# A last tile routed by expert in a second phase, in place of eight dense expert blocks over it

## The reference, cut to what matters

```
x = x + xattn(layernorm(x), ctx)          # x: 1024 x 128, ctx: 6404 x 128
n = layernorm(x)                          # 1024 tokens, 128 wide
expert_id = argmax(n @ wr + br)           # 8 experts
h = gelu(n @ w1[e] + b1[e])               # 128 -> 512, for the token's expert e
y = h @ w2[e] + b2[e]                     # 512 -> 128
out = x + y                               # only the chosen expert's y counts
```

## Time and profile before

| | before |
|---|---|
| median of the runs | 234.51 us |
| profiled execution, its own time | 234.7 us |
| span of that execution | 233.0 us |
| TensorE busy | 200.8 us, 86% |
| VectorE busy | 180.4 us, 77% |
| ScalarE busy | 157.9 us, 68% |
| GpSimd busy | 126.6 us, 54% |

### The profile page before, as it was taken

The page is one execution under the profiler, slowest core; times in us unless marked ns, Lnnn a source line. Parts: engine busy times, 40 slices in busy tenths (PEclk is TensorE's granted clock), DMA queues, the critical chain, the costliest instruction groups (busy, mean ns, idle before and its releaser), DMA issues.

```text
span 233.0 us, 5011 instructions
## 1 busy us (share of the span) xinstructions
PE 200.8 (86%) x1837; PEld 151.4 (65%) x1837; DVE 180.4 (77%) x395; ACT 157.9 (68%) x249; POOL 126.6 (54%) x177
## 2 busy tenths in 40 slices
PE   0289969999999999979989999899992899799970
PEld 0133436776866777746656777699981899789960
DVE  2999797697998997997995999957848437567770
ACT  2752899399399698699596799789332355766630
POOL 3695819708906808958608957655302730027783
PEclk9999985799999999999999999999996569999995
DMA  6999979979999999999989999989991559999100
GB/s 208 381 259 258 221 239 249 225 192 191 232 180 227 260 220 271 231 200 240 230 207 274 207 249 230 211 180 212 234 284 47 191 191 314 366 370 344 43 21 0
DMA packets 142958, 51.78 MB, mean 222 GB/s; under 512 B 121172, under 2 KB 140773, under 8 KB 142934
## 3 DMA queue, kind: packets, MB, share of 16 engines
q1 hardware_dynamic: 142000, 50.08, 92.8%
q0 software_dynamic: 784, 1.38, 1.7%
q10 hardware_dynamic: 150, 0.00, 0.0%
HBM read 10.74 MB, written 3.75 MB: 62 GB/s over the span
## 4 chain that ended last, share of the span: by engine, by line
PE 41%; DVE 23%; issue 13%; DMA 11%; POOL 6%; ACT 4%; SPq 1%; POOLq 0%; DVEq 0%; ACTq 0%
DMA PT<-Phl 9%; DVE S L798 6%; PE psX L1073 6%; PE psS L1055 5%; PE psS L1053 5%; PE psS L1054 5%; POOL out_x L606 5%; PE psO L1073 4%; DVE Phl L815 4%; PE psX L1075 3%; ACT S L649 3%; PE psO L1075 2%; PE psS L1279 2%; DMA S<-in_x 2%; PE psX L1084 2%
## 5 line engine op out<-in xcount | busy, mean ns | idle before, releaser
L649 ACT ACTIVATE S<-S,negb 128x1024 f32<-128x1024 f32 x48 | 55.0, 1145 | 17.5 <-DVE negb L806 17.5
L798 DVE TENSOR_SCALAR_CACHE_REDUCE S<-psS 128x1024 f32<-128x1024 f32 x48 | 58.2, 1216 | 9.9 <-PE psS L1055 9.8
L815 DVE TENSOR_TENSOR Phl<-S,Phl 128x1024 f16<-128x1024 f32 x38 | 51.5, 1354 | 5.3 <-ACT Phl L664 5.2
L531 POOL TENSOR_TENSOR Phl<-S,Phl 128x256 f16<-128x256 f32 x40 | 26.4, 691 | 52.2 <-ACT Phl L664 52.2
L664 ACT CAST Phl<-S 128x1024 f16<-128x1024 f32 x48 | 50.2, 1045 | 5.6 <-DMA PT<-Phl 4.2
L1053 PE MATMUL psS<-qT,gh 128*128 128x512 f16 x96 | 37.6, 392 | 5.6 <-DVE gl L776 3.0
L1073 PE MATMUL psO<-qn,PT 128*128 128x256 f16 x204 | 37.7, 279 | 0.7 <-DMA PT<-Phl 0.7
L1073 PE MATMUL psX<-qn,PT 128*128 128x256 f16 x204 | 36.4, 273 | 2.0 <-DMA PT<-Phl 2.0
L1055 PE MATMUL psS<-qT,gl 128*128 128x512 f16 x96 | 37.7, 393 | 0.0
L1054 PE MATMUL psS<-qT,gh 128*128 128x512 f16 x96 | 37.7, 393 | 0.0
L1075 PE MATMUL psO<-qn,PT 128*128 128x128 f16 x204 | 36.2, 223 | 0.0
(11 more groups left out here) (239 smaller groups left out, 426.3 us busy)
## 6 DMA issues: line engine op xcount, KB each, us to landing
PT<-wp SPq DMA_DIRECT2D x8, 512.0 KB, 6.0
stageT<-in_ctxT SPq DMA_DIRECT2D x6, 512.0 KB, 7.3
qn<-wp SPq DMA_DIRECT2D x6, 512.0 KB, 6.5
wp<-in_w SPq DMA_DIRECT2D x4, 512.0 KB, 4.8
stageT<-in_w SPq DMA_DIRECT2D x4, 512.0 KB, 4.8
rows_by_expert<-stageT SPq DMA_DIRECT2D x4, 385.5 KB, 5.3
PT<-Phl SPq DMA_TRANSPOSE x48, 4.2
S<-rows_by_expert SPq DMA_DIRECT2D x2, 258.0 KB, 5.9
```

The costliest lines, as they stand in the source:

```text
L531: last = nc.gpsimd.tensor_tensor(lo[:, r], slot(t, e)[:, r], hi[:, r], ALU.subtract)
L649: nc.scalar.activation(slot(t, e), slot(t, e), ACT.Exp, bias=negb[:, t:t + 1], accum_out=Lp[:, t * NG + e:t * NG + e + 1]).then_inc(exp_do ...
L798: nc.vector.tensor_scalar(out=into, in0=bank(u, n)[:, 0:into.shape[1]], scalar1=1.0 / GS, scalar2=None, op0=ALU.mult, op1=ALU.max, accum_o ...
L815: nc.vector.tensor_tensor(lo, slot(t, e), hi, ALU.subtract).then_inc(low_done, 1)
```

## The change

The dense blocks are removed. Tile 7 is dispatched like the others, but in a second phase, since its routing is known later. The first phase is as before. Then TensorE counts tile 7's choices on top of those of the first seven tiles, VectorE works out how many further blocks each expert now needs (`extra`), which rows of tile 7 fit into free rows of the blocks that are there and which go to added blocks behind them (`pos7`), and a second table of block owners (`bexp_all`). GpSimd sends tile 7 with an eighth scatter. There are NB = 8 + 8 - 1 = 15 blocks, all dispatched, and TensorE's loop has 15 instead of 22. SyncE now fetches four blocks' weights ahead (the first phase settles their owners) instead of two, then waits for the second phase (`experts_ready` 2), loads the other eleven registers, waits for both scatters' landings and reads the rows. The copy of tile 7 to a high and low half is gone, as are the constant `pick` and tile 7's own output DMA.

```diff
-    NB = TA + E - 1
-    NBLK = E + NB
-    FIRST = 2
+    NB = T + E - 1
+    FIRST = 4
...
             for b in range(FIRST):
                 fetch(b)
-            sp.reg_load(expert_reg[FIRST:NB], bexp[0:1, FIRST:NB])
+            sp.wait_ge(experts_ready, 2)
+            sp.reg_load(expert_reg[FIRST:NB], bexp_all[0:1, FIRST:NB])
...
             sp.wait_ge(rows_sent, 16 * TA)
+            sp.wait_ge(last_sent, 16)
             block_rows(0, 0, D, rows_landed)
             block_rows(1, 0, D, rows_landed)
...
+            pool.wait_ge(x2n_ready, H + 1)
+            pool.wait_ge(pos7_ready, 1)
+            pool.indirect_dma_start(out=xs, ..., in_=pay[:, TA, :], in_offset=None).then_inc(last_sent, 16)
...
             act.wait_ge(x7T_in_psum, 1)
-            nc.scalar.copy(xTp[:, 0, NB, :], x7T_psum).then_inc(x7T_high, 1)
-            act.wait_ge(x7T_low, 1)
             nc.scalar.copy(x2T[:, TA * P:N], x7T_psum).then_inc(x7T_ready, 1)
...
+            dve.wait_ge(router7_in_psum, 1)
+            io, first = best(router7_psum, TA, T)
+            nc.vector.tensor_tensor(oneh[:, TA:T, :], io, first, ALU.is_equal).then_inc(chosen7_ready, 1)
+
+            dve.wait_ge(ranks7_in_psum, 1)
+            link(...)    # 12 linked instructions of 1 to 64 columns: nall, extra, ahead, shift, place, over
+            nc.vector.tensor_copy(pos[:, TA:T], posf[:, TA:T]).then_inc(pos7_ready, 1)
+            link(...)    # 6 more, three of them on 120 columns: opened, worth, hit, fix
+            nc.vector.tensor_scalar(bexp_all[:, :], fix[:, :], float(E - 1), None, ALU.min).then_inc(experts_ready, 1)
...
+            for t in range(TA):
+                nc.tensor.matmul(both7_psum..., ones16[:, :], oneh[:, t, :]...broadcast_to([P, 2, E]), ...)
             pe.wait_ge(x2n_ready, H + 1)
             nc.tensor.transpose(x7T_psum, x2n[:, TA, :], idf[:, :]).then_inc(x7T_in_psum, 1)
...
+            pe.wait_ge(chosen7_ready, 1)
+            nc.tensor.matmul(rank7_psum, before[:, :], oneh[:, TA, :], ...)
+            nc.tensor.matmul(count7_psum, ones16[:, :], oneh[:, TA, :], ...).then_inc(ranks7_in_psum, 1)
...
             pe.wait_ge(w_low, T)
+            turn(0)
             up(0)
-            router_last()
+            turn(1)
             up(1)
-            for b in range(NBLK):
-                if b == E - 2:
-                    turn(0)
+            for b in range(NB):
                 for g, (s0, _) in enumerate(BATCHES):
-                    if g >= 2 and b == E + s0 - 5:
+                    if g >= 2 and b == s0 - 5:
                         turn(g)
-                if b + 2 < NBLK:
+                if b + 2 < NB:
                     up(b + 2)
-                if b == E - 2:
-                    turn(1)
                 down(b)
```

More of the change, by code:

```diff
@@ new lines, in _ @@
+            link(nc.vector.tensor_reduce(out=nall[:, :], in_=more[:, :, :], axis=AX.X, op=ALU.add))
+            link(nc.vector.tensor_tensor(extra[:, :], nall[:, :], nblk[:, :], ALU.subtract))
+            link(nc.vector.tensor_tensor(below[:, :, :], tri[:, :, :],
+                                         extra[:, :].unsqueeze(1).broadcast_to([P, E, E]), ALU.mult))
+            link(nc.vector.tensor_reduce(out=ahead[:, :], in_=below[:, :, :], axis=AX.X, op=ALU.add))
+            link(nc.vector.scalar_tensor_tensor(out=shift[:, :], in0=ahead[:, :], scalar=eblk[:, E - 1:E],
+                                                in1=eblk[:, :], op0=ALU.add, op1=ALU.subtract))
@@ new lines, in _ @@
+            link(nc.vector.tensor_tensor(place[:, :], rank7_psum, sblk[:, :], ALU.add))
+            link(nc.vector.tensor_tensor(over[:, :], place[:, :], eblk[:, :], ALU.is_ge))
+            link(nc.vector.tensor_tensor(over[:, :], over[:, :], shift[:, :], ALU.mult))
+            link(nc.vector.tensor_tensor(place[:, :], place[:, :], over[:, :], ALU.add))
+            link(nc.vector.tensor_tensor(place[:, :], place[:, :], oneh[:, TA, :], ALU.mult))
+            link(nc.vector.tensor_reduce(out=posf[:, TA:T], in_=place[:, :], axis=AX.X, op=ALU.add))
@@ new lines, in _ @@
+            nc.vector.tensor_copy(pos[:, TA:T], posf[:, TA:T]).then_inc(pos7_ready, 1)
+            link(nc.vector.tensor_scalar(opened[:, :], ahead[:, :], eblk[:, E - 1:E], None, ALU.add))
+            link(nc.vector.scalar_tensor_tensor(out=worth[:, :], in0=iota_e[:, :], scalar=-float(E), in1=extra[:, :],
+                                                op0=ALU.add, op1=ALU.mult))
+            link(nc.vector.tensor_tensor(hit[:, :, :], opened[:, :].unsqueeze(1).broadcast_to([P, NB, E]),
+                                         slot_no[:, :, :], ALU.is_equal))
@@ L1004, in finish @@
                 half, t = psY[b % RING][:, 0:D], yt[:, b % RING, :]
-                if b >= E:
-                    nc.vector.tensor_tensor(yf[:, b - E, :], half, t, ALU.add).then_inc(y_ready, 1)
-                    return
-                nc.vector.scalar_tensor_tensor(out=y7[:, b, :], in0=half, scalar=mask[:, b:b + 1], in1=t,
-                                               op0=ALU.mult, op1=ALU.add).then_inc(y_ready, 1)
-            for b in range(NBLK):
+                nc.vector.tensor_tensor(yf[:, b, :], half, t, ALU.add).then_inc(y_ready, 1)
+            for b in range(NB):
                 for g, (s0, _) in enumerate(BATCHES):
@@ L1209, in _ @@
             pe.wait_ge(chosen_ready, 1)
-            nc.tensor.matmul(rank_psum, before[:, :], oneh[:, :, :].rearrange("p t e -> p (t e)"),
+            nc.tensor.matmul(rank_psum, before[:, :], oneh[:, 0:TA, :].rearrange("p t e -> p (t e)"),
                              start=True, stop=False, skip_group_check=True)
```

155 lines of the change are left out of this document (71 added, 84 removed).

## The result

| | before | with the change |
|---|---|---|
| first set: median (executions) | 235.0 us (4) | 238.06 us (4), 237.85 to 239.54 |
| ratio, 95% interval | | 1.0137 [1.0092, 1.0183] |
| profiled execution, own time / span | 234.7 / 233.0 us | 238.18 / 236.4 us |
| four later sets of the same kernels | | 1.0101 [1.0045, 1.0157], 1.0022 [0.9993, 1.0051], 1.0076 [1.0036, 1.0115], 0.9990 [0.9955, 1.0025] |

What follows compares the result with a forecast made beforehand. TensorE's work after the blocks' start was taken as the bound: first `up` 197.55 + blocks 24.15 + transposes 1.2 + end wait 1.5 + clock 2.9 = 227.3 against 226.66, +0.65, so 235.2 us (range 233.6 to 237.0).

Steps and rivals of the forecast that it cites:

- the wait: On SyncE before the first read of rows: read at 192.9 us, not 191.3, 2.9 us later than before.
- the load itself: SyncE's second register load: 4.5 us for eleven registers, from 0.12 us plus 0.40 per register.
- the loss by the low clock: TensorE's first blocks at 1.2 GHz: half of 5.8 us lost, 2.9 us, against 4.35 before.
- Transpose to second table: From tile 7's transpose ending at 180.60 us through routing and VectorE's chain: `pos7` at 186.2, second owner table at 187.8.
- What does hold the rows is the load of registers: On SyncE: the register load, from 187.9 to 192.4 us, not the eighth scatter, decides when rows are read.
- lands at about 191.3: GpSimd's eighth scatter: starts at 188.82 us and lands at about 191.3, 1.3 us later than the seventh.
- The clock: TensorE at the first blocks: starts at 1.2 GHz, rises to 2.4 GHz 5.8 us later, by 203.4 us.
- rival 3: At the first blocks: clock rises early, 3.8 us after the first `up`, 1.9 us lost, 234.2 us; chance 0.12.
- The base: The profiled execution of the kernel before: last matmul ending at 226.66 us, against which the sum of 227.3 gave +0.65.
- No wait of TensorE from there: In the blocks, once the clock is at 2.4 GHz by 203.4 us: TensorE never waits, last matmul at 227.3.
- Rival 4: Rows or weights come late, tightest at `turn(2)`, rows landing 204.5 us, wanted 205.8; 3 us worse costs 1.7, 236.9; chance 0.05.

Runs made afterwards that it cites:

- before_again: The kernel before, unchanged, run again for a second trace: 234.19 us, ratio 1.0017.
- before_less_constants: The kernel before without the two GpSimd affine_selects of the constant `pick`: 234.62 us, ratio 1.0021.
- before_laid_out_as_after: The kernel before with two tables allocated in the changed kernel's larger sizes, so later addresses match it; no instruction changed: 234.93 us, ratio 1.0026.
- after_again: The changed kernel, unchanged, run again for a second trace: 236.31 us, ratio 1.0101 to the kernel before.
- after_third: The changed kernel, unchanged, run once more for the spread of its executions: 235.62 us, ratio 1.0022 to the kernel before.
- after_busy_up_to_first_block: The changed kernel with 45 unread matmuls before the first transposes of rows and 5 more between those and the first block: 234.82 us, ratio 0.9991.
- after_tensore_kept_busy: The changed kernel with 40 unread matmuls in TensorE's idle stretch before the first transposes of rows: 237.24 us, ratio 1.0056 to the kernel before.

## Why the prediction was wrong

The size of the change was near (+0.65 forecast, +0.9 over the later sets), in part by luck; the number on record was not, and five of its steps were off, two of them against each other. The step that failed first is the wait: not the load of registers but the scatter decided when the rows were read. Two terms were mis-sized on top of it: the load itself (4.5 us, measured 3.27) and the loss by the low clock (2.9 us, half of 5.8, where half of the measured 4.0 is 2.0).

- **Transpose to second table.** 5.6 us to `pos7` and 7.2 to the table were forecast from the transpose's end at 180.60; measured from 183.04, 5.7 (the copy at 188.55 took 0.15) and 7.5 (190.58). Right.
- **"What does hold the rows is the load of registers"** was wrong. It took 3.27 us, not 4.5, and the scatter decided. I had bound the load from below by 0.9 us, for the case that 4.91 was congestion, and had argued that away because 0.46 and 0.41 us per register agreed. Two points always agree with a line. Measured since: 2 registers 0.67 to 0.93 us, 4 registers 0.90 to 1.13, 9 registers 3.61 and 3.65, 11 registers 1.19, 1.42 and 3.2 to 3.3, 12 registers 4.9, 13 registers 3.12. Neither the count nor the traffic alone orders them. The Trainium skill's "DMA: Bandwidth & Descriptors", section "Latency and other measured facts", gives some 600 ns as the floor of a `tensor_load`; the shortest here, 0.67 us, lies just above it.
- **The scatter "lands at about 191.3".** +11.2 from the transpose; it was +12.1 to +12.5 in the five traces of the changed kernel and +10.9 with two fetches. It started at +8.3, where I had +8.7, and took 3.8 to 4.2 us, where I had 2.5. I had reckoned the four fetches' bytes against the read behind them, but not against the scatter in their midst. The two errors nearly cancel: the read came at +12.2 for +12.8 forecast, the first `up` at +16.9 for +17.4.
- **The clock** rose 4.0 us behind the first `up`, not 5.8; 3.7 to 4.0 in four traces of the kernel, 5.5 in the fifth. So rival 3's early rise came true in four of five. The Trainium skill's "TensorE: Matmul & The Clock Gate", section "What you observe", has around 4 us, and four of five traces agree. What I took for the rule, two rises of this trace at 5.8 and 5.9 us, was at the slow end of the spread.
- **The base.** The sum stands on one execution of before. Its layer was 52.9 us long, where before_again and before_less_constants have 51.3; there the first dispatched block stands 1.5 us sooner, which half of the time that the clock rose sooner would explain (3.2 us: 185.11 and 188.51 with transposes at 178.28 and 181.69, here 190.15 with 180.12). The windows of before_again and before_less_constants:

```profile
185.00:186.00 1.00, 1.00 (x16) 0.95 (x15) 0.00 (x0) 0.71 (x2) 0.70 (x2) 0.94 1.10 395
...
188.00:189.00 1.00, 1.00 (x15) 0.99 (x14) 0.00 (x0) 0.76 (x2) 0.81 (x1) 0.74 1.08 386
```

  In before_laid_out_as_after the clock rose as early, and TensorE lost 0.8 us behind ScalarE's late start. With the measured read and clock my sum gives 52.1 us from the transpose to the end, as after_again has (52.2) and only 0.1 over the average of before. The rest of the +0.9 comes in with the other traces, by the late clock of after_third and the late semaphores of after; so the near hit of +0.65 is in part errors that cancelled.
- **"No wait of TensorE from there"** fell in the first trace: blocks of 30.5 us against 28.8 without the late semaphores.
- **Rival 4** named the right place, `turn(2)`: with the clock up (after_busy_up_to_first_block) the rows landed at 204.5 and TensorE waited 2.83 us. That the time is the one I wrote, 204.5, is luck, since that trace's layer starts 0.7 us sooner. In after, with the clock low, TensorE's rows show no wait there.

What put the profiled execution 3.4 us over before is then mostly no step of the change: 2.45 us lie ahead of the transpose, and 1.7 in the late semaphores, against a forecast loss of clock that was 0.9 too high and a read 0.6 too late. Whether the other three executions of the first set had the same is not known: all four lie at 237.85 us or above, where only 6 of the 42 later ones do, and why they do so together stays open. My range had terms for the change alone and none for the spread of executions on either side, which the three times shown (234.11 to 235.48) hinted at less than it is: executions of the kernel before went from 231.3 to 237.9. What makes the semaphores late, what moves the attention part, and what a load of registers costs, stay open.

## What to carry to other kernels

Seven blocks fewer bought nothing: the first block now starts 17 us behind the transpose, where the dense ones started at 1.3, because they had filled the time in which the rows travel. Ask of work that is to go what it hides. Where one engine's wait is lifted, look at SyncE's queue next; here most of the clock's gain was lost to one read that stood late in it, and the gain of an early start to a load of registers in it. And a forecast of under 1% needs the spread of several traces, not one trace's sum.

## What I had not expected of the hardware

- The same load of 11 registers took 1.19 us behind two reads of rows and 3.27 behind four fetches of 512 KB; yet 13 registers took 3.12 with the DMA engines 0.18 to 0.37 busy, and 9 took 3.6.
- A scatter of 128 rows landed 2.5 to 2.6 us after its start behind two fetches of 512 KB or four of 256 KB, 3.8 to 4.2 behind four of 512 KB.
- The clock fell 3.4 us after full work had ended, with about 1 us of matmuls in between, and took 3.4 us to come back (after_tensore_kept_busy: 194.5, 197.9, 201.3). It did not fall in the 2.8 us that TensorE stood in after_busy_up_to_first_block.
- ScalarE and VectorE can start 1.7 to 2.7 us behind the end of TensorE's row that they wait for: at the eighth block in four traces of after and its variants (not in the four others of after itself), at the ninth and thirteenth in one each, and at the third dense block in two of four traces of the kernel before.
